# Scan stage of a Mamba-2 mixer: convolution taps ahead of the state steps, a tanh and a weight split between the decay exponentials, skip factors on ScalarE

## The reference

```python
proj = jnp.einsum('bsd,od->bso', h, in_proj_w)
gate, hBC, dt = ...                                  # 8192, 8192 + 2*8*128, 128 columns
hBC = jax.nn.silu(causal_conv(hBC, conv_w, conv_b))  # 4 taps along the sequence
hid, B, C = ...                                      # 128 heads of 64; 8 groups of 128
D_res = Dp[None, None, :, None] * hid                # the skip
M = jnp.einsum('bcihn,bcjhn->bcijh', Ch, Bh) * L     # within chunks of 128
Y_diag = jnp.einsum('bcijh,bcjhp->bcihp', M, hc)
states = jnp.einsum('bclhn,bhcl,bclhp->bchpn', Bh, decay_states, hc)
prev_states = ...                                    # states carried over chunks
Y_off = jnp.einsum('bclhn,bchpn,bhcl->bclhp', Ch, prev_states, jnp.exp(A_cs))
y = (Y_diag + Y_off) + D_res
yg = y * jax.nn.silu(gate)                           # then RMS norm over each group
out = jnp.einsum('bsd,od->bso', y, out_proj_w)
```

## Time and profile before

| | us |
|---|---|
| median of 3 runs (lowest, highest) | 1970.82 (1969.7, 1971.56) |
| the profiled execution, its own time | 1970.32 |
| its span | 1968.5 |
| outside the span | 1.82 |
| busy: PE | 1916.5 (97%) |
| busy: PEld | 1552.6 (79%) |
| busy: DVE | 1545.0 (78%) |
| busy: ACT | 1621.1 (82%) |
| busy: POOL | 1512.0 (77%) |
| mean granted TensorE clock | 0.995 |

### The profile page before, as it was taken

One profiled execution on the slowest core, in us unless ns is written; L12 is line 12 of the kernel. 1 busy time (PEld: TensorE's weight loads), 2 busy tenths in 40 slices (PEclk: granted clock), 3 DMA queues, 4 the chain that ended last, 5 costly groups with the idle time before them and its releaser, 6 DMA issues.

```text
span 1968.5 us, 32828 instructions
## 1 busy us (share of the span) xinstructions
PE 1916.5 (97%) x10675; PEld 1552.6 (79%) x10675; DVE 1545.0 (78%) x2806; ACT 1621.1 (82%) x3256; POOL 1512.0 (77%) x1102
## 2 busy tenths in 40 slices
PE   8999999999999999999999999999999999999998
PEld 6574667777888888888888888888888888888876
DVE  8787899866777777777777777777777777787878
ACT  5354877657898989898989898989889898989896
POOL 5644667647888888888888888878788787878887
PEclk9999999999999999999999999999999999999999
DMA  5625323543343343434333333434343433443333
GB/s 207 198 64 147 101 87 117 167 165 118 111 121 118 111 124 106 127 103 128 114 115 121 108 122 107 133 102 137 106 129 104 130 112 118 122 149 122 118 102 124
DMA packets 114474, 241.74 MB, mean 123 GB/s; under 512 B 23681, under 2 KB 24706, under 8 KB 113794
## 3 DMA queue, kind: packets, MB, share of 16 engines
q1 hardware_dynamic: 110466, 227.06, 37.3%
q0 software_dynamic: 3840, 12.59, 2.3%
HBM read 226.75 MB, written 12.85 MB: 122 GB/s over the span
## 4 chain that ended last, share of the span: by engine, by line
PE 39%; DVE 16%; ACT 15%; issue 6%; POOL 3%; DMA 1%; SPq 0%; ACTq 0%; DVEq 0%; POOLq 0%
PE ps L75 11%; PE ps L77 10%; PE ps L76 10%; DVE s_cv L2467 8%; ACT s_lm L2215 4%; PE ps L2130 4%; DVE s_state L2425 2%; ACT ps L2254 2%; PE ps L2138 2%; ACT s_cv L2248 2%; PE ps L2077 1%; POOL w_lo L2726 1%; ACT s_hid L2282 1%; DMA gu_s<-group_dram 1%; ACT s_y_hi L2268 1%
## 5 line engine op out<-in xcount | busy, mean ns | idle before, releaser
L75 PE MATMUL ps<-h_hi,w_hi 128*128 128x512 f32 x1168 | 477.4, 409 | 2.7 <-POOL w_hi L890 1.6
L2726 POOL TENSOR_TENSOR w_lo<-w_raw,w_hi 128x1024 fp32r<-128x1024 f32 x142 | 338.8, 2394 | 174.5 <-ACT w_hi L2198 174.5
L76 PE MATMUL ps<-h_lo,w_hi 128*128 128x512 f32 x1168 | 456.4, 391 | 0.0
L2467 DVE SCALAR_TENSOR_TENSOR s_cv<-ps,s_par,s_cv 128x511 f32<-128x511 f32 (+2 forms) x480 | 358.7, 747 | 124.5 <-ACT s_cv L2248 113.2
L77 PE MATMUL ps<-h_hi,w_lo 128*128 128x512 f32 x1152 | 451.5, 392 | 0.0
L2752 POOL TENSOR_TENSOR s_lm<-s_lm,s_cbt 128x512 f32<-128x512 f32 x256 | 327.7, 1307 | 12.6 <-ACT s_lm L2230 10.2
L2215 ACT ACTIVATE s_lm<-s_rows,s_steps 128x128 f32<-128x128 f32 x1024 | 324.6, 390 | 9.5 <-PE ps L2130 9.5
L75 PEld LDWEIGHTS ps<-h_hi,w_hi 128*128 128x128 f32 x1168 | 219.9, 188 | 55.1 <-issue 6.2
L77 PEld LDWEIGHTS ps<-h_hi,w_lo 128*128 128x128 f32 x1152 | 216.3, 188 | 48.5
L76 PEld LDWEIGHTS ps<-h_lo,w_hi 128*128 128x128 f32 x1168 | 220.6, 189 | 40.0 <-issue 0.2
L75 PE MATMUL ps<-s_wo_hi,s_y_hi 128*128 128x512 f32 x512 | 203.8, 398 | 3.7 <-DVE s_y_lo L2559 3.7
(11 more groups left out here) (339 smaller groups left out, 4425.5 us busy)
## 6 DMA issues: line engine op xcount, KB each, us to landing
w_raw<-in_w_in SPq DMA_DIRECT2D x144, 512.0 KB, 3.7
s_rows<-acs_dram SPq DMA_DIRECT2D x256, 256.0 KB, 3.6
s_wo_raw<-in_w_out SPq DMA_DIRECT2D x128, 256.0 KB, 3.4
w_raw<-in_gu_q SPq DMA_DIRECT2D x14, 512.0 KB, 3.7
f_d_q<-in_d_q SPq DMA_DIRECT2D x28, 256.0 KB, 2.7
f_d_w<-in_d_s SPq DMA_DIRECT2D x28, 256.0 KB, 3.4
table<-shifted SPq DMA_DIRECT2D x16, 256.0 KB, 3.0
xs<-in_x SPq DMA_DIRECT2D x8, 256.0 KB, 6.1
```

The costliest lines, as they stand in the source:

```text
L75: nc.tensor.matmul(dst, l_hi, r_hi, start=start, stop=False)
L76: nc.tensor.matmul(dst, l_hi, r_lo, start=False, stop=False)
L2467: nc.vector.scalar_tensor_tensor(dst, src[:, 0:SEQ - d], par[:, v.b, 4 * j + 3 - d:4 * j + 4 - d], dst, ALU.mult, ALU.add).then_inc(conv_c ...
L2726: nc.gpsimd.tensor_tensor(w_lo[:, slot, :], w_raw[:, slot, :], w_hi[:, slot, :].bitcast(F32), ALU.subtract).then_inc(w_lo_ready, 1)
```

## The change

Five moves, none of which alters what is computed.

In slot 0 VectorE does the taps of tile b right after those of tile a, then the state steps, and then both finishes. Before, the finish of a and the state steps stood between the taps. In slot 1 the taps of the C tile come ahead of the state steps. In slot 0 ScalarE does tanh of b and the split of the late weight tile between the scale of a and the scale of b; before both scales came first, then the split, then the tanh. The skip factors are made by ScalarE (at the end of slot 1, and once in the opening stage).

```diff
+        def act_skip(act, v):
+            act.wait_ge(par_loaded[v.b], 48 * (v.g + 1))
+            nc.scalar.activation(skip4[:, v.b], par[:, v.b, 50:58], ACT.Copy, scale=4.0).then_inc(skip_ready, 1)
...
@@ act_first
+                if k == 2:
+                    act_skip(act, v)
@@ act_double
                 act_tap(act, v, B_AT, b_bank)
                 act_tanh(act, v, B_AT, b_bank)
+                act_skip(act, v)
                 return
             if s == 3:
                 act_tanh(act, v, tile_of(b), h_b)
             act_scale(act, ua, a_on)
+            if not s:
+                act_tanh(act, v, tile_of(b), h_b)
+                act_w(act, *load_unit(un, LATE[s]))
             act_scale(act, ub, b_on)
-            if load_unit(un, LATE[s]):
+            if s and load_unit(un, LATE[s]):
                 act_w(act, *load_unit(un, LATE[s]))
             if s == 3:
                 act_rms(act, un)
-            else:
+            if s == 2:
                 act_tanh(act, v, tile_of(b), h_b)
@@ dve_first
-                if k == 3:
-                    dve_skip(dve, v)
@@ dve_double
             if s == 0:
                 dve_tile(dve, v, tile_of(a), h[0])
+                dve_tile(dve, v, tile_of(b), h[1])
+                state()
                 dve_silu(dve, v, tile_of(a), h[0])
-                state()
-                dve_tile(dve, v, tile_of(b), h[1])
                 dve_silu(dve, v, tile_of(b), h[1])
             elif s == 1:
                 c_bank, b_bank = bank(un, ("H", 1, C_AT)), bank(un, ("H", 1, B_AT))
                 dve_tile(dve, v, tile_of(b), h[1])
                 dve_silu(dve, v, tile_of(b), h[1])
+                dve_tile(dve, v, C_AT, c_bank)
                 state()
-                dve_skip(dve, v)
-                dve_tile(dve, v, C_AT, c_bank)
                 dve_silu(dve, v, C_AT, c_bank)
                 dve_tile(dve, v, B_AT, b_bank)
                 dve_silu(dve, v, B_AT, b_bank)
```

More of the change, by code:

```diff
@@ L2489, in dve_bt @@
             nc.vector.tensor_copy(b_l[:].rearrange("p c n -> p (c n)"), src[:, 0:3 * P]).then_inc(took["BT"], 1)
-        def dve_skip(dve, v):
-            dve.wait_ge(par_loaded[v.b], 48 * (v.g + 1))
-            nc.vector.tensor_scalar(skip4[:, v.b], par[:, v.b, 50:58], 4.0, None, ALU.mult).then_inc(skip_ready, 1)
         def dve_ssq(dve, v, src):
```

## The result

The changed kernel takes 1946.96 us (median of 5 runs, 1946.07 to 1949.97), the kernel before 1970.53 in the same comparison (5 runs, 1969.58 to 1971.56). The ratio is 0.9884 with a 95% interval of 0.9874 to 0.9894, so 23.6 us are gone where 21.8 were forecast (1970.8 to 1949). The profiled execution took 1946.96 with a span of 1945.0.

A forecast was written before the change was run, and what follows sets the result against it. TensorE was taken as the bound, losing time at two waits for bank B: 14 x 0.56 + 15 x 0.96 = 22.2 us off 1970.3 gives 1948.1, forecast as 1949. Own range 1946 to 1952; 8-in-10 range 1946 to 1960.

The forecast's parts named there:

- What bounds the kernel: Scan stage: TensorE, busy 93.92 of 95.00 us, sets the pace and loses time at two DIAG waits for PSUM bank B.
- Starts, not idle times: TensorE's two turns: loss sized by distances between starts, 0.56 and 0.96 us, 22.2 in all, not the 16.2 idle.
- Slot 0, VectorE: Slot 0: with taps and state covering two tanh waits, the finish of b comes 1.8 us earlier, done at 1062.5.
- Slot 0, ScalarE: Slot 0: ScalarE gains 0.8 to 0.9 us; late weight's low part ends at 1064.0, before G a wants it at 1064.8.
- The margin of the state: Slot 0: the state of a is complete about 1060.9, OFF a starts at 1061.45, a margin of 0.5 us.
- Slot 1: Turn from slot 1 to 2: B's taps start at 1087.1, all 0.96 us goes, 0.3 to 0.4 to spare.
- The skip step: Slot 1: leaving VectorE saves 0.16 us start to start; on ScalarE it costs nothing, at most 8.1 us if uncovered.
- One wait staying: Rival: one bank B wait remains; 1962.5 us if slot 1 yields nothing, 1955.9 if slot 0 does; chance 0.2.
- Another engine as the pace: Rival: a ScalarE to VectorE to ScalarE chain holds the 95 us period, so nothing is gained, 1970.8 us; chance 0.06.
- The late state: Rival: slot 0's state, behind the taps of b, delays OFF a and slows the kernel, for example 1978 us; chance 0.08.

The follow-up runs named there:

- act_order_back: Changed kernel with ScalarE's slot 0 order as before (both scales, late split, tanh of b): ratio 0.9877 to the kernel before, scan 1402.0 us.
- finish_a_first: Changed kernel with the finish of a ahead of slot 0's state steps: ratio 0.9926 to the kernel before, scan 1410.7 us.
- state_last: Changed kernel with slot 0's state steps behind both finishes: ratio 1.0087 to the kernel before, scan 1440.4 us.
- skip_on_dve: Changed kernel with the skip factors made by VectorE again, right behind slot 1's state steps: ratio 0.9945 to the kernel before, scan 1414.9 us.
- skip_in_wait: Changed kernel with the skip factors made by VectorE between B's taps and B's finish: ratio 0.9887 to the kernel before, scan 1400.3 us.
- split_behind_scales: Changed kernel with only tanh of b between the scales, the late weight split behind both: ratio 0.9920 to the kernel before, scan 1410.5 us.

## Why the prediction was right, point by point

**What bounds the kernel** held: TensorE's two waits for bank B were all that recurred. With both gone its rows fill a unit, and every kernel that was slower than the change had a wait in TensorE's rows that came back in 14 or 15 units. TensorE is busy for 98.2% of the span, forecast above 98. The length of a unit was misread: 95.00 us is the scan length divided by 15, and its first interval is short. A unit was 96.31 and is 94.75, not 93.5. Only the difference enters the sum, so nothing followed from it.

**Starts, not idle times** held. TensorE's starts show 22.7 us gone from the two kinds of turn, where 22.2 were forecast and the idle rows had 16.2. The counts held too: in the kernel before, 14 turns from slot 0 to 1 lost 0.54 to 0.59 and the first of them 0.15. The two profiled executions differ by 23.4 us; the 0.7 that lie outside these turns were not followed up. They are part of why the median came 2 us below the forecast of 1949, together with the small amount by which the gain was rounded down for the edges, without a row to go by.

**Slot 0, VectorE** held to 0.1 us: finishes done 7.73 after the first tap, worked out as 7.8.

**Slot 0, ScalarE.** The times were right (tanh, split, scale in the forecast order, low part 0.6 ahead of G a instead of 0.8). The step by which the low part in the old order is "0.2 ahead of the new start and too near" was not: act_order_back runs with that order and loses 0.3 us in all. What is true is narrower: the old order leaves the low part no margin at all but costs 0.02 us a turn, and with the tanh moved and the split not, 8.5 us are lost.

**The margin of the state** was mis-read, "the state of a is complete two steps before the end" with a margin of 0.5: OFF a needs both, and the margin is 1052.32 - 1052.07 = 0.25 us, which finish_a_first used up. It did not change the result.

**Slot 1** held: B's taps at 1077.95 are 9.15 earlier than the 1087.1 worked out, and the taps of a in slot 0 are 9.14 earlier than in the earlier trace rows. The margin was put at 0.3 to 0.4; it is 0.4 to 0.5.

**The skip step** is the term that was mis-sized. Its removal was counted as 0.16 us from VectorE, the copy on ScalarE as nothing. The second is right. The first holds only for the order of before: behind the new place of the state it meets GpSimd's `w_lo`, and left there it would have taken 12.9 of the 23.1 us back. The sum came out right because the change moved the step away as well, and for this part that is luck: the prediction had no reason for the move but the 0.16.

**Rivals.** One wait staying: it did not; forced by leaving one slot as it was, it costs 8.5 (slot 1 left) or 9.2 us (slot 0 left) against the change, not the 14.4 and 7.8 of the rival. Of the 14.4 the lead from slot 0 takes away nearly half; the 9.2 is near its 7.8. Another engine as the pace: no. The late state: the mechanism is real. Forced in state_last, it cost 38.4 us where 22 were expected for that run: each turn lost 2.06 and not 1.5, since OFF a needs both states and a fresh start is paid for, and in five turns the clock fell.

## What to carry to other kernels

When one engine is busy nearly all the time, list the few waits in its rows that come back each period, and size each by the distance between starts at an undisturbed and a disturbed place, not by the idle time shown. Put a step that another engine is not waiting for behind one whose partner needs time (taps of the next tile while the tanh of the last runs), and then check what each moved instruction now runs beside and which of its neighbours' margins it uses. A lead won in one stage pays for waits in the next, so single edits' gains do not add up, and an edit can be needed only because of its neighbour.

## What the runs showed of the hardware

- A VectorE scaling of 128x8 from SBUF to SBUF took 1.39 us when GpSimd's 128x1024 subtraction was already running, 0.25 when the last fifth of a 128x512 product was left to run, and 0.16 when nothing was; it ended 0.03 us behind GpSimd's instruction in all 31 cases in the three traces (before, skip_on_dve, skip_in_wait). A reduction of the same 8 columns took 0.15 during such a subtraction.
- A wait of TensorE of 1.8 us was followed in 5 units of 14 by most of 4 us at the lower clock (0.62 and 0.53 granted in two windows of 2 us). At the start of the scan a wait of 3.5 us goes with a drop in 13 of the 14 traces. No wait of 0.2 to 0.9 us in the scan of any kernel does.
- Ahead of 128-column matmuls such short waits cost 0.2 to 0.3 us beyond the idle time shown (0.34 shown and 0.56 lost, 0.74 and 0.96); ahead of a 512-column one it was 0.1 (0.53 and 0.63, split_behind_scales).
